# Softmax denominators of a fused attention and feed-forward kernel: summed at every row of a head and inverted by ScalarE

## The reference

```
qp = ln(x) @ Wq;  kp = ctx @ Wk;  vp = ctx @ Wv          # 8 heads of 32
attn = softmax(qh @ kh^T * 32**-0.5)                      # over the 120 context rows
x = x + (attn @ vh) @ Wo + bo
x = x + bitlinear(ln(gelu(bitlinear(ln(ln(x)), w1, b1))), w2, b2)
# bitlinear: rows quantised to 8 bits, weights to -1, 0, 1
```

## Time and profile before

| what | value |
|---|---|
| span of the profiled execution | 1090.8 us |
| median of three timed executions | 1093.15 us |
| TensorE matmuls busy | 954.2 us, 87% |
| VectorE busy | 1021.3 us, 94% |
| ScalarE busy | 925.1 us, 85% |
| GpSimd busy | 723.0 us, 66% |
| mean granted TensorE clock | 0.986 |

### The profile page before, as it was taken

How to read it: one execution, slowest core, us unless ns; L and a number is a source line. 1 busy time by engine, 2 the same in 40 slices (tenths; PEclk the granted TensorE clock), 3 DMA queues, 4 the chain that set the end, 5 groups by cost and what they waited for, 6 DMA issues and landing times.

```text
span 1090.8 us, 29867 instructions
## 1 busy us (share of the span) xinstructions
PE 954.2 (87%) x9616; PEld 648.1 (59%) x9651; DVE 1021.3 (94%) x1399; ACT 925.1 (85%) x2590; POOL 723.0 (66%) x1056
## 2 busy tenths in 40 slices
PE   6999999999999999999998567877777777877776
PEld 4777777777777777777775344444444444444444
DVE  2799999999999999999999999999999999999997
ACT  5788888888888888888877869999999999999993
POOL 4266666776666666666676577777777777777776
PEclk9999999999999999999999889999999999999998
DMA  6589987686666666556655103322332233323334
GB/s 169 137 178 186 183 165 161 162 160 160 162 160 161 157 162 157 160 155 164 163 133 127 39 20 40 39 30 37 38 38 33 34 38 38 37 30 38 38 40 68
DMA packets 145144, 114.60 MB, mean 105 GB/s; under 512 B 52376, under 2 KB 135576, under 8 KB 145072
## 3 DMA queue, kind: packets, MB, share of 16 engines
q1 hardware_dynamic: 127488, 96.77, 37.3%
q0 software_dynamic: 16864, 16.26, 12.4%
q10 hardware_dynamic: 720, 0.66, 0.2%
HBM read 71.62 MB, written 33.63 MB: 96 GB/s over the span
## 4 chain that ended last, share of the span: by engine, by line
DVE 37%; PE 31%; issue 26%; DMA 3%; POOL 1%; DVEq 1%; ACT 1%; SPq 1%; ACTq 0%; POOLq 0%
DVE gn_low L859 7%; DVE gn_high L859 7%; PE banks L1437 6%; PE banks L1428 6%; DVE nm_part L746 4%; PE banks L1337 4%; PE banks L1381 3%; PE banks L1390 3%; DVE gn_low L845 2%; PE banks L1412 2%; DVE gn_high L845 2%; DVE h L800 2%; DVE inv_sum L774 2%; PE banks L1402 2%; DVE h L793 2%
## 5 line engine op out<-in xcount | busy, mean ns | idle before, releaser
L1060 ACT ACTIVATE probs<-banks 120x512 f32<-120x512 f32 x256 | 132.2, 602 | 43.0 <-PE banks L1367 43.0
L746 DVE TRANSPOSE_TENSOR_REDUCE nm_part<-banks 128x64 f16<-128x2048 f32 x64 | 147.9, 2312 | 2.5 <-PE banks L1337 2.2
L1108 ACT ACTIVATE g_dev<-g,g_sum 128x1024 bf16<-128x1024 f32 x128 | 149.1, 1165 | 0.0
L1113 ACT ACTIVATE g<-banks,h_dq 128x1024 f32<-128x1024 f32 x128 | 142.5, 1131 | 3.4 <-PE banks L1270 3.2
L1437 PE MATMUL banks<-wo_sb,o_t 128*128 128x256 f32 x512 | 135.0, 399 | 1.5 <-DVE o_t L888 1.2
L1300 PE MATMUL banks<-w_t,g_t 128*128 128x256 bf16 x1008 | 123.2, 276 | 13.1 <-ACT g_t L1146 10.2
L1300 PEld LDWEIGHTS banks<-w_t,g_t 128*128 128x128 f16 x1008 | 94.8, 99 | 51.5 <-issue 28.2
L1264 PE MATMUL banks<-w_t,h_t 128*128 128x512 bf16 x471 | 118.2, 388 | 3.7 <-ACT g L1113 1.7
L1428 PE MATMUL banks<-xt,wq_c 128*128 128x256 f32 x512 | 121.3, 380 | 0.0
L544 POOL COPY h_dq<-h_cl 128x2 f32<-128x2 f32 (+1 forms) x64 | 13.7, 215 | 149.9 <-DVE h_qs L814 148.8
L622 POOL TENSOR_TENSOR g_r<-g_ve,neg_half 128x2 f32<-128x2 f32 x64 | 105.9, 1654 | 1.3 <-ACT g_ve L1129 1.3
(11 more groups left out here) (184 smaller groups left out, 2715.2 us busy)
## 6 DMA issues: line engine op xcount, KB each, us to landing
x_in<-in_x SPq DMA_DIRECT2D x64, 256.0 KB, 4.5
xt<-in_x_t SPq DMA_DIRECT2D x64, 256.0 KB, 4.0
xr<-in_x SPq DMA_DIRECT2D x64, 256.0 KB, 4.3
out<-xr SPq DMA_DIRECT2D x64, 256.0 KB, 4.7
out<-res POOLq DMA_DIRECT2D x62, 256.0 KB, 4.4
ctx_t<-in_ctx_t SPq DMA_DIRECT2D x64, 128.0 KB, 3.4
r_bc<-r_rows SPq DMA_DIRECT2D x63, 128.0 KB, 4.1
w_raw<-in_w_t SPq DMA_DIRECT2D x8, 256.0 KB, 6.4
```

The lines of the kernel that those rows point to most:

```text
L746: dve.tensor_reduce(nm_part[:, :, 0:C * RB], blocks_p, AX.X, ALU.max, negate=True, apply_transpose=True).then_inc(max_done, 1)
L1060: act.activation(probs[:, p, j, :, :], sc_p[0:KV, j, :, :], ACT.Exp, scale=SCALE).then_inc(probs_done, 1)
L1108: act.activation(g_dev[:, t, :], g[:, p, t, :], ACT.Square, scale=-float(F), bias=g_sum[:, p, t:t + 1], accum_out=g_ssq[:, p, t:t + 1]).th ...
L1113: act.activation(g[:, p, t, :], u_p[t], ACT.Gelu, scale=h_dq[:, b, t:t + 1], accum_out=g_sum[:, p, t:t + 1]).then_inc(gelu_done, 1)
```

## The change

`sums` multiplies the exponentials by an all-ones operand of 32 columns, so that each head's sum appears at all 32 partitions of the head in a tile of 128x512, the shape of the weighted values: 8 matmuls of 256 columns. ScalarE takes the logarithm of this tile out of PSUM and then the exponential of its negative; VectorE multiplies the weighted values, straight from bank 1, with it. The compact inverse, the two 16-bit halves, the spread and the copy of the weighted values are gone, with the operands that they needed. The sums now come before the values on TensorE; the output projection shares bank 0 with the sums (before: bank 1 with the values), so it waits for the logarithm. A table set of ScalarE that has both functions is asked for at the start.

```diff
-        y_p = bank[1].rearrange("p (t n) -> p t n", t=T)
-        sum_p = bank[0][:, 0:P]
-        spread_p = bank[0].rearrange("p (c n) -> p c n", c=C)
+        y_p = bank[0].rearrange("p (t n) -> p t n", t=T)
+        sum_p = bank[0].rearrange("p (c n) -> p c n", c=C)
         o_p = bank[1].rearrange("p (c n) -> p c n", c=C)
...
+        log_sum = sb("log_sum", [P, C, ROWS], scope=late_mem)
+        inv_sum = sb("inv_sum", [P, C, ROWS], scope=late_mem)
...
+                def weigh(b, p):
+                    after(dve, y_ps, b - 1)
+                    dve.wait_ge(o_ps, b + 1)
+                    dve.wait_ge(inv_done, b + 1)
+                    dve.tensor_tensor(o_t[:, p, :, :], o_p, inv_sum[:, :, :], ALU.mult).then_inc(on_done, 1)
...
-                        dve.reciprocal(inv_sum[:, q, :], sum_p).then_inc(inv_done, 1)
...
-                        dve.scalar_tensor_tensor(out=inv_part[:, q, :], in0=inv_hi[:, q, :], scalar=part_sign[:, 0:1],
-                                                 in1=inv_sum[:, q, :], op0=ALU.mult, op1=ALU.add).then_inc(split_done, 1)
...
-                        dve.tensor_tensor(o_t[:, q, :, :], spread_p, o_raw[:, q, :, :], ALU.mult).then_inc(on_done, 1)
+                        weigh(b, q)
...
+                act.preload_act_table_set("natural_log_exp_and_others")
...
-                def copy_o(b, p):
...
-                def high_half(b, p):
...
+                def logarithms(b):
+                    act.wait_ge(sum_ps, b + 1)
+                    act.activation(log_sum[:, :, :], sum_p, ACT.Ln).then_inc(log_done, 1)
+
+                def inverses(b):
+                    after(act, on_done, b)
+                    act.wait_ge(log_done, b + 1)
+                    act.activation(inv_sum[:, :, :], log_sum[:, :, :], ACT.Exp, scale=-1.0).then_inc(inv_done, 1)
...
                     if live(i - 1, NB):
-                        copy_o(i - 1, q)
+                        logarithms(i - 1)
+                        inverses(i - 1)
...
-                    if live(i - 1, NB):
-                        high_half(i - 1, q)
...
                 steps(act, A0, NB, L0, L1, attn, 4, aside)
+                logarithms(NB - 1)
+                inverses(NB - 1)
                 act.activation(table[:, :], ones[:, 0:1], ACT.Gelu)
-                copy_o(NB - 1, 1)
...
                 def values(b, r):
-                    after(pe, x1_done, b - 1)
+                    after(pe, on_done, b)
                     pe.wait_ge(v_done, b + 1)
-                    pe.wait_ge(probs_done, 4 * (b + 1))
...
                 def sums(b, p):
-                    after(pe, on_done, b)
+                    after(pe, x1_done, b - 1)
+                    pe.wait_ge(probs_done, 4 * (b + 1))
                     for c in range(C):
-                        for t in range(T):
-                            for j in range(HC):
-                                last = pe.matmul(sum_p[strip(j), :], sum_sel[0:KV, c * T + t, :],
-                                                 probs[:, p, j, c, t * P:(t + 1) * P],
...
+                        for j in range(HC):
+                            last = pe.matmul(sum_p[strip(j), c, :], ones[0:KV, 0:HD], probs[:, p, j, c, :],
+                                             start=True, stop=True, skip_group_check=True)
...
                     if t == 0:
-                        pe.wait_ge(o_done, left(b + 2))
+                        pe.wait_ge(log_done, left(b + 2))
                         pe.wait_ge(on_done, b + 1)
...
                     if live(i - 1, NB):
+                        sums(i - 1, q)
                         values(i - 1, (n + 3) % 4)
-                        sums(i - 1, q)
...
-                    if live(i - 1, NB):
-                        spread_inverses(i - 1, q)
```

More of the change, by code:

```diff
@@ L80, in xattn_ffn @@
         ones = sb("ones", [P, P])
[L82 to L86, removed]
         head_map = sb("head_map", [P, C, HC, RB])
@@ L199, in xattn_ffn @@
         nmt_first_p = bank[0][:, ROWS:ROWS + P // 2].bitcast(F16)
-        nmt_second_p = bank[1][:, 0:P // 2].bitcast(F16)
+        nmt_second_p = bank[0][:, 0:P // 2].bitcast(F16)
         nmt_p = bank[3][:, 0:P // 2].bitcast(F16)
@@ L463, in _ @@
                 pool.memset(head_map[:, :, :, :], 0.0).then_inc(s_map, 1)
-                pool.memset(part_sel[:, :], 0.0).then_inc(s_map, 1)
-                pool.memset(spread[:, :, :, :], 0.0).then_inc(s_map, 1)
-                pool.wait_ge(s_map, 3)
+                pool.wait_ge(s_map, 1)
                 pool.affine_select(out=head_map[:, :, :, :], in_=head_map[:, :, :, :], compare_op=ALU.not_equal, fill=1.0,
                                    base=0, pattern=[[-RB, C], [-32, HC], [-1, RB]], channel_multiplier=1).then_inc(s_map, 1)
[L469 to L475, removed]
                 pool.wait_ge(s_const, N_CONST)
@@ L673, in _ @@
                 dve.memset(neg_one[:, :], -HALF_ONE).then_inc(s_const, 1)
-                dve.memset(sum_sel[:, :, :], 0.0).then_inc(s_sel, 1)
                 dve.memset(nm_part[:, :, :], 0.0).then_inc(s_sel, 1)
-                dve.wait_ge(s_sel, 2)
-                for c in range(C * T):
-                    dve.memset(sum_sel[:, c, SR * c:SR * (c + 1)], SUM_SCALE).then_inc(s_const, 1)
+                dve.wait_ge(s_sel, 1)
                 dve.wait_ge(wq_sum, 1)
@@ L701, in mean_magnitude @@
                     dve.wait_ge(mag_sum, 1)
-                    dve.tensor_scalar(w_mean[:, :], bank[1][:, 0:2], 1.0 / (F * D), CLIP, ALU.mult, ALU.max).then_inc(mean_done, 1)
+                    dve.tensor_scalar(w_mean[:, :], bank[0][:, 0:2], 1.0 / (F * D), CLIP, ALU.mult, ALU.max).then_inc(mean_done, 1)
                     dve.wait_ge(mean_done, 1)
@@ L1240, in sum_magnitudes @@
                     for n in range(2):
-                        last = pe.matmul(bank[1][:, 0:2], ones[:, :], w_abs[:, n, :], start=(n == 0), stop=(n == 1))
+                        last = pe.matmul(bank[0][:, 0:2], ones[:, :], w_abs[:, n, :], start=(n == 0), stop=(n == 1))
                     last.then_inc(mag_sum, 1)
@@ L1413, in keys @@
                                   start=False, stop=(m == C - 1), skip_group_check=True)
-                def spread_inverses(b, p):
-                    pe.wait_ge(split_done, b + 1)
-                    for c in range(C):
-                        for t in range(T):
-                            last = pe.matmul(spread_p[:, c, t * P:(t + 1) * P],
-                                             spread[:, c * T + t, :, :].rearrange("p j n -> p (j n)"),
-                                             inv_part[:, p, :], start=True, stop=True)
-                    last.then_inc(spread_ps, 1)
                 def queries(b, p):
@@ L1496, in _ @@
                 pe.wait_ge(probs_done, 4 * NB)
+                sums(NB - 1, 1)
                 values(NB - 1, 3)
-                sums(NB - 1, 1)
                 first_rows_up(1)
@@ L1502, in _ @@
                 turn_bias(2)
-                spread_inverses(NB - 1, 1)
                 rows_up(1, 1)
```

76 lines of the change are left out of this document (14 added, 62 removed).

## The result

The changed kernel takes 1081.55 us (median; 1080.39 to 1084.61) where the kernel before takes 1093.09 in the same session: a ratio of 0.9903, interval 0.9889 to 0.9916, 11.5 us faster. The forecast was 1079.5, with a range of 1066 to 1092. On two other chips the same pair gave 0.9948 (0.9925 to 0.9971) and 0.992 (0.9891 to 0.9949), so only 5.4 and 6.3 us between the medians, with the changed kernel's runs there spread from 1078.3 to 1094.9. That spread is a part of the result; the last experiment bears on it.

A forecast was written before the change was run, and what follows sets the result against it. TensorE and VectorE were taken as balanced, a step shortening only as far as both do. Gains 13.2 + 0.7 - 0.3 = 13.6 us took the span from 1090.8 to 1077.2, about 1079.5 with 2.35 around it; range 1066 to 1092.

The forecast's parts named there:

- TensorE paces, VectorE's 1.11 us are worth nothing beyond it: Loop step: TensorE goes from 9.00 to 8.78 us; VectorE's larger saving of 1.11 us adds nothing more.
- The spread gives 0.22, not 0.31: TensorE, queries to scores: removing the spread saves 0.22 us a step; the other 0.09, a tiling-mode change, stays.
- Logarithm and exponential 0.60 each, cover of 0.59 nearly used: ScalarE's step: two new functions at 0.60 us each, net 0.47 more, leaving some 0.1 of 0.59 us idle.
- Rival (c): Slower: the logarithm takes longer than a copy, decisive from 0.82 us on; at 1.20 us, 1116 us total; 9 in 100.
- The values' wait for the product has 0.5 us spare: TensorE's values wait for VectorE's product of the batch before, which should be over more than 0.5 us earlier.
- rival (b): No change: the values wait for VectorE's late product, which eats the 0.22 us a step; 1092 us; 10 in 100.
- 60 steps, 13.2 us: Loop from batch 2 to 62: 60 x (9.00 - 8.78) = 13.2 us gained.
- The 0.07 above the plain step: Loop average of 9.07 us against a plain 9.00: some longer steps, left as they are.
- Start -0.3, end +0.7: Table load before the first weight DMAs costs 0.3 us; VectorE's removed work at the last step gains 0.7.
- The second part has none of the changed work: 0: Kernel's second part, after the batch loop: no gain or loss, 0 us.
- Around the span 2.35 us: Time between the profiled span of 1090.8 us and the median of 1093.15, added to the predicted span.
- Rival (d), the tables: Logarithm and exponential served by different sets: two table loads of 1.28 us each step; 1197 us; 2 in 100.

The follow-up runs named there:

- the last experiment: Changed kernel, but from batch 4 on the row-scale load reads batch 1's long-stored row without waiting for its own store: 1079.4 us, ratio 0.9856.

## Why the prediction was right, point by point

- **TensorE paces, VectorE's 1.11 us are worth nothing beyond it.** Right. The step went from 9.01 to 8.75, forecast 9.00 to 8.78; TensorE's added 0.43 came through whole, VectorE's added 0.95 for 0.14. VectorE is idle for 1.13 us a step (12.86% of 8.75); about 0.9 was forecast.
- **The spread gives 0.22, not 0.31.** Right: queries to scores is 1.82 now. The Trainium skill's rule in "TensorEngine Tiling (Array Packing)", Key Properties, that a change of tiling mode drains the engine, stands here: no drain went, and the trace agrees in so far as the change of mode is 0.09 dearer: 1.82 to the scores, 1.73 to the spread of the same mode before. The kernel before without its spread, with all of VectorE's work, has 1.82 too (428.11 - 426.29).
- **The projection is held by the logarithm.** Right: 0.98 after the values, forecast 0.99, with the weight load's 0.41 us put down to `log_sum`.
- **Logarithm and exponential 0.60 each, cover of 0.59 nearly used.** Right: 0.60 and 0.63 us, and ScalarE's busy time per step went from 7.57 (84.07% of 9.01) to 8.00 (91.48% of 8.75), +0.43 where 0.47 was worked out. Rival (c) needed 0.82. In the same paragraph 416.34 stands in no row; the scores of rows 4 start at 416.56, 0.98 after the exponentials' end, not 0.76. Nothing else uses it.
- **The values' wait for the product has 0.5 us spare.** Right in plain steps: the product is over at 409.01, the values start at 409.50. In a long step it is not, and there rival (b)'s wait does appear, as a follower of late queries:

```profile
133.96 0.69 DVE L793 TENSOR_TENSOR q_t<-banks,r_bc 128x512 f32<-128x512 f32 x1 [1.78 <-DMA r_bc<-r_rows]
```

```profile
135.31 1.07 PE L1322 MATMUL banks<-probs,v_sb 120*32 120x256 f32 x16 [1.04 <-DVE o_t L741]
```

- **60 steps, 13.2 us.** Right in size, 14.29, but as two terms: the plain steps gave 60 x 0.26 = 15.6 and the excess took 1.3 back. "The 0.07 above the plain step ... I leave as they are" was the weak sentence, and that it cost so little on the first chip was luck: measured against the 3.8 of the one profile of the kernel before, the excess would have taken back 5.6 (9.4 - 3.8) and 7.6 on the other two. The kernel before has no profile on those chips, so what it took there is not known. The round trip did not get faster with the step: a load of row scales lands after 4.1 us (median) in both kernels.
- **Start -0.3, end +0.7.** Mis-sized by little. The first weight DMA does not wait for the table load: it is issued at 0.88 us while the table loads (0.86 before). The first product starts 0.20 later (4.99 for 4.79), yet the maxima of batch 2 come 0.19 earlier; on the other two chips they come at 37.44 and 36.94, so this term lies within the spread. The end gave 0.41; why not more, no run says. The low end of the gain in the sum, 9, is 9.6 by its own terms (60 x 0.17 + 0.7 - 1.28).
- **"The second part has none of the changed work: 0."** This step failed, by 3.35 us. Its steps are equal within 0.1, but the diff renames one wait of GpSimd at the handover, from `split_done` to `on_done`, and that wait was not priced; the cost that the prediction did see there, the last logarithm and inverse ahead of the table load, turned out to be nothing. The addition behind the renamed wait starts 4.75 us later against the last maxima (16.28 - 11.53).
- **Around the span 2.35 us.** 1.5 in the profiled run after (1081.3 - 1079.8); the 2.35 mixed the median with another run's span. The span was missed by +2.6 (1079.8 for 1077.2): handover +3.35, rest +0.64, end +0.29, against -1.1 for the 60 steps, -0.5 for the start and -0.1 for the second part. With -0.85 around the span this makes 1081.3 for 1079.5. That the total came within 2 us is partly luck: the handover's miss stands against the smaller misses, and on the other two chips the changed kernel took 1088.84 and 1087.91.
- **Chain still on TensorE.** Not to be told: the chain of the profile after ends within the second part.
- **Rival (d), the tables.** Two table loads in all, as forecast. Its argument from placement by the longest run was turned round: one set serves logarithm and exponential, so the longest run speaks against (d). Without the request each step held two loads all the same; how they are placed stays open.

## What to carry to other kernels

When two engines are level, price both and take the later; relief of one alone gave 0.03 and 0.11 us a step here, of both 0.26. Read the diff for renamed waits, too: when the semaphore of removed work is replaced by one that comes later, the engine that waits on it at a change of phase pays for it, 3.35 us here. After shortening a loop, check the round trips that don't shrink with it, here a 1 KB store and its load, and time the kernel on more than one chip before giving the gain a number.

## What the hardware showed unexpectedly

A store of 1 KB kept its load waiting for 0.78 us in one step and 4.58 in another, and whole runs of the one changed kernel lie between 1078 and 1095 us while its plain step, 8.75, is the same to the hundredth on all three chips. How much of that is this store is open beyond the last experiment. The logarithm took as long as a copy of the same tile (0.60 us), and a load of tables took 1.28 us with the activation 0.02 behind it.
